# Per-tile centring and scaling on GpSimd, reciprocal roots by Newton steps for four streams at once, and the bias within the weights

## The reference

```python
def step(h, _):
    h = h + 0.01 * jnp.tanh(h)
    h = h * jax.nn.sigmoid(h)
    h = _layernorm(h, ln_w, ln_b)        # (h - mean) * rsqrt(var + 1e-5) * w + bias
    h = jnp.einsum('bsc,dc->bsd', h, W) + b
    return (h, None)
x, _ = jax.lax.scan(step, x, None, length=N_ITERS)   # N_ITERS = 30
```

## Time and profile before

| what | value |
|---|---|
| time, median of 3 runs | 2552.14 us (2551.59 to 2553.27) |
| profiled execution | 2566.49 us, span 2564.7 us |
| PE busy | 2378.7 us, 93% |
| PEld busy | 2320.6 us, 90% |
| DVE busy | 2081.9 us, 81% |
| POOL busy | 2027.5 us, 79% |
| ACT busy | 1811.9 us, 71% |
| L1094 products of the iterations, PE | 7680 matmuls, 275 ns each |
| L512 roots, POOL | 480, 1636 ns each |
| L515 scaling, POOL | 480, 1475 ns each |
| L661 statistics, DVE | 1920, 418 ns each |
| L704 state update, DVE | 464, 1209 ns each |
| L683 scaling, DVE | 960, 372 ns each |
| L957, L964, L967, ACT | 480, 464, 480; 1012, 1037, 1068 ns each |

### The profile page before, as it was taken

One profiled execution on the slowest core, in us unless ns is written; L12 is line 12 of the kernel. 1 busy time (PEld: TensorE's weight loads), 2 busy tenths in 40 slices (PEclk: granted clock), 3 DMA queues, 4 the chain that ended last, 5 costly groups with the idle time before them and its releaser, 6 DMA issues.

```text
span 2564.7 us, 60894 instructions
## 1 busy us (share of the span) xinstructions
PE 2378.7 (93%) x19678; PEld 2320.6 (90%) x19935; DVE 2081.9 (81%) x5761; ACT 1811.9 (71%) x2185; POOL 2027.5 (79%) x1592
## 2 busy tenths in 40 slices
PE   6829999999999999999999999999862999999998
PEld 5829999999999999999999999989861999999998
DVE  5999999999999999999999999987572444444443
ACT  3779999999999999999999999833210334344333
POOL 4769999999999999999999999995764444444443
PEclk9969999999999999999999999999885999999999
DMA  9100000000000000000000000003223555555554
GB/s 261 69 1 1 0 0 0 0 0 0 0 0 0 0 0 0 0 0 0 0 0 0 0 0 0 0 18 110 75 73 109 212 216 212 211 214 216 212 212 148
DMA packets 121574, 164.56 MB, mean 64 GB/s; under 512 B 14982, under 2 KB 74018, under 8 KB 121360
## 3 DMA queue, kind: packets, MB, share of 16 engines
q1 hardware_dynamic: 111792, 145.12, 16.6%
q0 software_dynamic: 9088, 17.14, 2.0%
q10 hardware_dynamic: 608, 1.30, 0.2%
HBM read 40.40 MB, written 24.65 MB: 25 GB/s over the span
## 4 chain that ended last, share of the span: by engine, by line
DVE 58%; PE 31%; issue 7%; POOL 1%; DMA 1%; ACT 1%; SPq 1%; another core or an unknown queue 0%; DVEq 0%; POOLq 0%; ACTq 0%
DVE pair_stats L661 25%; DVE state L704 18%; PE psum L1265 11%; PE psum L1256 11%; DVE state L683 6%; PE psum L1094 5%; PE psum L1084 2%; DVE it_vars L665 2%; DVE x_stats L661 1%; POOL sorted_rows L556 1%; DVE resid L731 1%; PE psum L1213 1%; DMA sorted_rows<-state,slot 1%; PE psum L1246 1%; DVE state L700 1%
## 5 line engine op out<-in xcount | busy, mean ns | idle before, releaser
L1094 PEld LDWEIGHTS psum<-w_ffn,turned 128*128 128x128 f32 x7680 | 1010.1, 192 | 36.0
L1094 PE MATMUL psum<-w_ffn,turned 128*128 128x128 f32 x7680 | 1013.7, 275 | 12.8 <-issue 0.2
L512 POOL TENSOR_TENSOR it_rstd<-it_vars,minus_half 128x8 f32<-128x8 f32 x480 | 785.5, 1636 | 0.0
L515 POOL TENSOR_TENSOR state<-state,it_rstd 128x768 f32<-128x768 f32 x480 | 708.0, 1475 | 37.6
L661 DVE BATCH_NORM_STATS2 pair_stats<-state 128x6 f32<-128x256 f32 x1920 | 685.1, 418 | 0.0
L1084 PE MATMUL psum<-ident,state 128*128 128x128 f32 x4352 | 595.6, 281 | 59.1 <-DVE state L700 42.8
L704 DVE SCALAR_TENSOR_TENSOR state<-state,psum 128x1024 f32<-128x1024 f32 x464 | 560.8, 1209 | 1.8 <-ACT state L964 0.9
L1084 PEld LDWEIGHTS psum<-ident,state 128*128 128x128 f32 x4352 | 479.5, 143 | 78.0 <-issue 57.7
L957 ACT COPY turned<-psum 128x1024 f32<-128x1024 f32 x480 | 485.8, 1012 | 80.4 <-PE psum L1084 43.9
L967 ACT ACTIVATE state<-state 128x1024 f32<-128x1024 f32 x480 | 512.7, 1068 | 28.6 <-DVE state L700 9.1
L964 ACT ACTIVATE state<-psum 128x1024 f32<-128x1024 f32 x464 | 481.0, 1037 | 0.0
(11 more groups left out here) (190 smaller groups left out, 1725.2 us busy)
## 6 DMA issues: line engine op xcount, KB each, us to landing
adjT<-resid SPq DMA_DIRECT2D x312, 320.0 KB
adjT<-sorted_rows SPq DMA_DIRECT2D x156, 66.5 KB, 1.8
resid<-in_x_dram SPq DMA_DIRECT2D x16, 512.0 KB, 7.3
state<-in_adj_dram SPq DMA_DIRECT2D x16, 512.0 KB, 7.3
adjT_dram<-adjT SPq DMA_DIRECT2D x7, 512.0 KB, 3.7
adjT<-adjT_dram SPq DMA_DIRECT2D x7, 512.0 KB, 3.5
out_dram<-resid,adjT POOLq DMA_INDIRECT x156, 2.4
sorted_rows<-state,slot POOLq DMA_INDIRECT x128
```

The lines of the kernel that those rows point to most:

```text
L512: nc.gpsimd.tensor_tensor(it_rstd[s % 8][:, :], it_vars[s % 4][:, :], minus_half[:, 0:TILES], ALU.pow).then_inc(it_pow, 1)
L515: nc.gpsimd.tensor_tensor(values[s][:, 0:POOL_TILES, :], values[s][:, 0:POOL_TILES, :], wide(it_rstd[s % 8][:, 0:POOL_TILES]), ALU.mult).t ...
L1094: last = nc.tensor.matmul(dst[:, t, :], stationary(t), moving(t), start=bias is None and m == 0, stop=m == len(terms) - 1, skip_group_chec ...
```

## The change

The statistics are kept in one tile for all 16 streams (`it_moments`), and `variance` and L683 go from DVE's iteration. POOL now works in batches of four streams. It waits for the statistics of all four, and computes the reciprocal roots of 4 x 8 = 32 columns at once from the sum of squares: one addition of 128 x eps, one multiplication by -0.5/128, a first guess by integer arithmetic on the bits, then three Newton steps of four instructions. That is 15 instructions, 14 of which have a wait for their own completion behind them. A one-column instruction (`pool_tick`) follows. Then each of the 8 tiles of each of the four streams gets one `tensor_scalar` with two per-row operands, subtract the mean and multiply by the root: 32 instructions of 128x128.

The bias matmuls of the iterations go. Instead, the copy after the transposition adds 1.0 to every value, and the bias / 128 is added to every row of the weights: the 128 ones then sum the bias, the ones times the centred weights sum to zero, and the centred rows times the constant bias / 128 sum to zero as well. For odd streams DVE copies tiles 0 to 3 of the eight and ACT the other four; even streams stay with ACT. PE waits for DVE's part too when the stream is odd.

```diff
-        SILU_LAG, STATS_LAG, SCALE_LAG, FLIP_LAG, EVAC_LAG = 1, 2, 5, STREAMS - 3, STREAMS - 2
-        POOL_TILES = 6
+        SILU_LAG, STATS_LAG, FLIP_LAG, EVAC_LAG = 1, 2, STREAMS - 3, STREAMS - 2
...
-            def iteration(base):
-                for s in range(STREAMS):
-                    pool.wait_ge(it_var, base + (s + 1))
-                    nc.gpsimd.tensor_tensor(it_rstd[s % 8][:, :], it_vars[s % 4][:, :], minus_half[:, 0:TILES],
-                                            ALU.pow).then_inc(it_pow, 1)
-                    pool.wait_ge(it_pow, base + (s + 1))
-                    nc.gpsimd.tensor_tensor(values[s][:, 0:POOL_TILES, :], values[s][:, 0:POOL_TILES, :],
-                                            wide(it_rstd[s % 8][:, 0:POOL_TILES]), ALU.mult).then_inc(it_scaled, 1)
+            ROOT_STEPS = 15
+
+            def roots(b, first):
+                v, h = it_vars[b % 2][:, 0, :], it_vars[b % 2][:, 1, :]
+                y, w = it_rstd[b % 2][:, :], it_work[b % 2][:, :]
+                at = [0]
+
+                def linked(ins):
+                    at[0] += 1
+                    ins.then_inc(it_root, 1)
+                    pool.wait_ge(it_root, first + (b * ROOT_STEPS + at[0]))
+
+                squares = it_moments[:, BATCH * b:BATCH * (b + 1), :, :].rearrange("p s i (h e) -> p (s i) h e", h=2)
+                linked(nc.gpsimd.tensor_tensor(halves(v), squares[:, :, :, 2], halves(root_const[:, 0, :]), ALU.add))
+                nc.gpsimd.tensor_tensor(h, v, root_const[:, 1, :], ALU.mult).then_inc(it_root, 1)
+                at[0] += 1
+                linked(nc.gpsimd.tensor_scalar(y.bitcast(I32), v.bitcast(I32), -0.5,
+                                               float(0x5f3759df + (7 << 22)), ALU.mult, ALU.add))
+                for _ in range(3):
+                    linked(nc.gpsimd.tensor_tensor(w, y, y, ALU.mult))
+                    linked(nc.gpsimd.tensor_tensor(w, w, h, ALU.mult))
+                    linked(nc.gpsimd.tensor_tensor(w, w, root_const[:, 2, :], ALU.add))
+                    linked(nc.gpsimd.tensor_tensor(y, y, w, ALU.mult))
+                assert at[0] == ROOT_STEPS
+
+                nc.gpsimd.tensor_tensor(pool_tick[:, :], minus_one[:, 0:1], minus_one[:, 0:1], ALU.mult)
+
+            def iteration(base, first):
+                for b in range(STREAMS // BATCH):
+                    pool.wait_ge(it_stats, base + BATCH * (b + 1))
+                    roots(b, first)
+                    for j in range(BATCH):
+                        s = BATCH * b + j
+                        for t in range(TILES):
+                            at = 3 * (t % 2) + 1
+                            mean = it_moments[:, s, t // 2, at:at + 1]
+                            root = it_rstd[b % 2][:, TILES * j + t:TILES * j + t + 1]
+                            last = nc.gpsimd.tensor_scalar(values[s][:, t, :], values[s][:, t, :], mean, root,
+                                                           ALU.subtract, ALU.mult)
+                        last.then_inc(it_scaled, 1)
...
+            nc.vector.scalar_tensor_tensor(w_ffn[:, :], crow[:, 1, 0:D], 1.0 / D, w_ffn[:, :], ALU.mult, ALU.add)
...
                     if n is not None:
                         dve.wait_ge(silu_done, n + 1)
-                        statistics(pair_stats[s % 4], values[s]).then_inc(it_stats, 1)
-                    if m is not None:
-                        dve.wait_ge(it_pow, m + 1)
-                        for t in range(POOL_TILES, TILES):
-                            last = nc.vector.tensor_scalar(values[r][:, t, :], values[r][:, t, :],
-                                                           it_rstd[r % 8][:, t:t + 1], None, ALU.mult)
-                        last.then_inc(it_scaled_v, 1)
-                    if n is not None:
-                        dve.wait_ge(it_stats, n + 1)
-                        variance(it_vars[s % 4][:, :], pair_stats[s % 4]).then_inc(it_var, 1)
+                        statistics(it_moments[:, s], values[s]).then_inc(it_stats, 1)
+                    if m is not None and r % 2 == 1:
+                        dve.wait_ge(it_flip, m + 1)
+                        nc.vector.tensor_scalar(turned[r % 4][:, 0:4, :], ring[r % 4][:, 0:4, :], 1.0, None, ALU.add
+                                                ).then_inc(it_turned_v, 2)
...
-                        nc.scalar.copy(turned[s % 4], ring[s % 4]).then_inc(it_turned, 1)
+                        own = slice(0, TILES) if s % 2 == 0 else slice(4, TILES)
+                        nc.scalar.activation(turned[s % 4][:, own, :], ring[s % 4][:, own, :], ACT.Copy, bias=1.0
+                                             ).then_inc(it_turned, 1)
...
                         pe.wait_ge(it_scaled, n + 1)
-                        pe.wait_ge(it_scaled_v, n + 1)
...
                         pe.wait_ge(it_turned, m + 1)
-                        rows(ring[r % 4], [(lambda t: turned[r % 4][:, t, :], lambda t: w_ffn[:, :])], bias=0
+                        if r % 2 == 1:
+                            pe.wait_ge(it_turned_v, m + 1)
+                        rows(ring[r % 4], [(lambda t: turned[r % 4][:, t, :], lambda t: w_ffn[:, :])]
                              ).then_inc(product, 1)
```

More of the change, by code:

```diff
@@ L108, in network @@
         shift = [sb(f"shift{j}", [P, 2, TILES]) for j in range(4)]
-        it_vars = [sb(f"it_vars{j}", [P, TILES]) for j in range(4)]
-        it_rstd = [sb(f"it_rstd{j}", [P, TILES]) for j in range(8)]
+        BATCH = 4
+        it_moments = sb("it_moments", [P, STREAMS, TILES // 2, 6])
+        it_vars = [sb(f"it_vars{j}", [P, 2, BATCH * TILES]) for j in range(2)]
+        it_rstd = [sb(f"it_rstd{j}", [P, BATCH * TILES]) for j in range(2)]
+        it_work = [sb(f"it_work{j}", [P, BATCH * TILES]) for j in range(2)]
+        root_const = sb("root_const", [P, 3, BATCH * TILES])
+        pool_tick = sb("pool_tick", [P, 1])
         row_vars = [sb(f"row_vars{j}", [P, TILES]) for j in range(4)]
@@ L161, in network @@
         h_bias = sb("h_bias", [P, 3, GW], BF16)
-        bias_mv = [sb(f"bias_mv{j}", [P, 4, P], BF16) for j in range(2)]
+        bias_mv = sb("bias_mv", [P, 4, P], BF16)
         def part(t, first, n):
@@ L468, in _ @@
             nc.gpsimd.memset(h_bias[:, :, :], 0.0)
-            for j in range(2):
-                nc.gpsimd.memset(bias_mv[j][:, :, :], 0.0)
+            nc.gpsimd.memset(bias_mv[:, :, :], 0.0)
+            nc.gpsimd.memset(root_const[:, 0, :], D * EPS)
+            nc.gpsimd.memset(root_const[:, 1, :], -0.5 / D)
+            nc.gpsimd.memset(root_const[:, 2, :], 1.5)
             nc.gpsimd.memset(mean_mat, 1.0 / D)
@@ L523, in _ @@
+            iteration(0, 0)
+            with pool.Fori(1, ITERS, 1) as i:
+                iteration(i * STREAMS, i * (STREAMS // BATCH * ROOT_STEPS))
             first = 0
@@ L648, in _ @@
                                       cpart[row, piece, 0, :].unsqueeze(1).to_broadcast([1, 3, GW]))
-                for j in range(2):
-                    last = nc.vector.tensor_copy(bias_mv[j][row, :, :],
-                                                 cpart[row, piece, 1 + j, 0:D].unsqueeze(1).to_broadcast([1, 4, P]))
+                last = nc.vector.tensor_copy(bias_mv[row, :, :],
+                                             cpart[row, piece, 2, 0:D].unsqueeze(1).to_broadcast([1, 4, P]))
             link(last)
@@ L1085, in flip, with rows @@
                 return last
-            def rows(dst, terms, bias=None):
+            def rows(dst, terms, bias=False):
                 for bank in range(2):
-                    if bias is not None:
-                        nc.tensor.matmul(dst[:, 4 * bank:4 * bank + 4, :], ones_bf[:, :], bias_mv[bias][:, :, :],
+                    if bias:
+                        nc.tensor.matmul(dst[:, 4 * bank:4 * bank + 4, :], ones_bf[:, :], bias_mv[:, :, :],
                                          start=True, stop=False, skip_group_check=True)
@@ L1094, in rows @@
                             last = nc.tensor.matmul(dst[:, t, :], stationary(t), moving(t),
-                                                    start=bias is None and m == 0, stop=m == len(terms) - 1,
+                                                    start=not bias and m == 0, stop=m == len(terms) - 1,
                                                     skip_group_check=True)
@@ L1202, in _ @@
                     rows(psM, [(lambda t: turned[d % 3][:, t, :], lambda t: w_mix[:, 0, :]),
-                               (lambda t: mask[:, t, :], lambda t: values[d][:, t, :])], bias=1).then_inc(mix_psum, 1)
+                               (lambda t: mask[:, t, :], lambda t: values[d][:, t, :])], bias=True).then_inc(mix_psum, 1)
                 if f is not None:
```

10 lines of the change are left out of this document (3 added, 7 removed).

## The result

The changed kernel takes 4626.0 us (median of 4 runs, 4624.4 to 4626.9), the kernel before 2551.9 in the same comparison: ratio 1.813, 95% interval 1.811 to 1.816. Forecast were 2690 us within 2430 to 3150: the sign is right, the size is far outside the range.

What follows compares the result with a forecast made beforehand. POOL was taken to bound the kernel before and after: 120 batches of 4.8 + 32 x 0.28 us, less 1510.3, plus 3.5, less 6.7, give +137.7 on 2552.1, so 2690 us, range 2430 to 3150.

Steps and rivals of the forecast that it cites:

- the price of the tile instruction: POOL's 128x128 tensor_scalar, taken as 0.28 us from the affine select's 0.25 plus 0.03 for two pointers.
- Ends 0.14 and 0.39: Limits for the tile instruction's spacing: a MEMSET's 0.14 us below, ACT's same-shaped instruction with two pointers, 0.39, above.
- T: Start-to-start spacing of POOL's 128x128 tensor_scalar instructions, forecast at 0.28 us; each 0.01 us is 38 us of time.
- (b): Rival, much slower: each pointer operand costs POOL a fetch before the tile; 0.39 us spacing, 3113 us; chance 0.21 with (d).
- POOL bounds the kernel before: In the iterations POOL holds the period at 3.14 us a slot (one stream, one iteration), three engines just behind.
- Roots of a batch: POOL's fifteen root instructions and one tick per four streams: 4.8 us, fourteen links 0.32 us apart.
- PE without the bias 2.65 us a slot, DVE 2.78, the half copy 0.6: Relieved engines per slot: PE 3.09 less 0.44, DVE 1.35 + 1.13 + 0.30; half copy every other slot.
- Start +3.5, end -6.7: Ends of POOL's iterations: first batch waits for four streams' statistics, +3.5 us; spare time before router products absorbs 6.7.
- A batch comes in time: POOL's batch has 7 and 10 slots, over 22 us, before PE's transposes need its first and last streams.
- Rival (a): Faster: tile instruction cheaper than any reading one in the trace, spacing below 0.244 us; about 2460 us, floor 2376; chance 0.27.
- Rival (d): PE's clock drops to 1.2 GHz as PE is busy 77%; +1030 us if held throughout; chance 0.21 with (b).

Runs made afterwards that it cites:

- f3: Kernel before with the batched Newton roots alone, POOL scaling seven tiles by one tensor_tensor, DVE one, nine slots behind; bias matmuls stay: 2559.1 us against 2566.4, ratio 0.997.
- g2: Kernel before with batched Newton roots, all eight tiles scaled on POOL, two Newton steps instead of three: 2524.4 us against 2552.2, ratio 0.989.
- f4: Changed kernel with only tile 0 of each stream centred and scaled on POOL, the other seven left as they are: 2383.2 us against 2566.4 before.
- e4: Changed kernel with each tile instruction handling only 64 of its 128 columns, both pointers kept: 3796.3 us.
- f1: Changed kernel with one two-operation tensor_scalar of 128x1024 with constants per stream instead of eight of 128x128 with pointers: 3394.8 us against 2566.4 before.
- h1: Changed kernel with one single-operation tensor_scalar of 128x1024 (multiply by constant 1.0) per stream instead of eight of 128x128: 2965.4 us.
- e1: Changed kernel with constants 0.0 and 1.0 instead of the mean and root pointers in the tile instruction: 3984.1 us.

## Why the prediction was wrong

The step that failed is the price of the tile instruction, "I take 0.28: the row of the same engine and width, and 0.03 for the pointers", with its ends, "Ends 0.14 and 0.39". T is 0.774. A batch has 32 of them and there are 120 batches, so this one term is (0.774 - 0.28) x 3840 = 1897 us of the 1936 that the forecast missed. The mechanism was right: POOL stays the bound, and its batches set the time. The size of one term of the sum was not. The runs put in its place

T = 0.18 fixed + 0.083 per pointer + columns x 2.5 ns (one operation) or x 3.4 ns (two),

which meets all seven measured values within 0.05 us (the 128-column ones within 0.01).

For 128 columns: 0.18 + 0.17 + 0.43 = 0.78. Of the 0.49 missed, about 0.14 are the pointers beyond the 0.03 allowed, 0.33 are the columns (0.43 against the 0.10 that the select's 0.25 leaves over the fixed 0.147), and the rest is the fixed part. What went wrong in the reasoning: the column's price was carried over from instructions that do other things (a MEMSET reads nothing, the select keeps a value or puts a constant), and the upper bound was built from tensor_tensor at 1.65 ns, as if one input must cost less than two. It costs more. Rows that disagree on a price by a factor of more than two (0.14, 0.25, 0.36, 0.39) were taken for a bracket, while the operation itself had never been seen on this engine. No rival had a dear column in it: (b), the nearest, stopped at 3113 us. Why one input with an operation is slower than two inputs stays open, and so does why the root part's own tensor_scalar (32 columns, integers, constants) lasts only 0.22 us.

Point by point:

- POOL bounds the kernel before: borne out, though hardly alone. With less work on POOL the slot fell from 3.14 only to 3.12 (f3, where DVE has no gap) and 3.09 (g2, where PE has none); the most that was gained is 28 us.
- Roots of a batch: 4.8 forecast, 4.95 measured. Links 0.33 apart instead of 0.32, in the first iteration, where the waits are against constants, as in the later ones, where they are against a register: the register costs nothing visible.
- PE without the bias 2.65 us a slot, DVE 2.78, the half copy 0.6: in f4 PE measured 2.67, DVE 2.77 and the half copy 0.59 from start to start. Right.
- Start +3.5, end -6.7: measured +1.6 and +4.8. Wrong in sign at the end: the prediction looked for what the new copies on DVE wait for in the middle of the iterations, and not at the wait ahead of them in the last one (DVE 68.33 us, PE 52.73). With the first batch, 9.5 us too long, it is some 20 us in 2074.
- A batch comes in time: right, POOL waits for statistics once, 3.54 us ahead of its first batch.
- Rival (b), pointers: it exists, 0.083 us each, and is a fifth of T. The rule of the Trainium skill, "GPSIMD Engine Reference", section Performance pitfalls for Q7 kernels, on small read commands (about 102 cycles, an estimated 0.085 us at its 1.2 GHz) has the same size; the page states it for reads such as one per gather index, and that a pointer operand is such a read no run shows. The same page of the Trainium skill, section Engine selection, says that one-input operations run roughly at line rate; that doesn't hold for this instruction: 3.4 and 2.5 ns a column (e4, f1, h1) would be an estimated 4 and 3 cycles at that clock, and both are above the 1.65 ns of two inputs. The measurement decides.
- Rival (a): nowhere near. Its floor, 176 us less, was met by f4 (183 less), once seven eighths of the tile work are gone.
- Rival (d), PE's clock: it did fall, to a granted 0.78, with PE busy 54% of the stretch, not the 77% at 1.00 that were forecast. It isn't in the loss, since PE waited over 3 us for POOL ahead of its transposes (3.32 and 3.33 above).

## What to carry to other kernels

When the whole sum hangs on the price of one operation that the trace doesn't show on that engine, rows of other operations are not bounds, not even a neighbouring one with more inputs; widen the range by a factor, or measure that one instruction first. Replacing one long instruction by eight short ones with per-row operands multiplies fixed and pointer costs by eight on an engine with no room; here that is 0.35 of each 0.774, and the price of the columns is the rest. And the gain of relieved engines (here 0.38 us a slot) is only what the new work on the bounding engine leaves of it.

## What the runs showed of the hardware that was not expected

- On GpSimd a tensor_scalar of float32 costs 2.5 ns a column with one operation and 3.4 with two, where tensor_tensor, one of its inputs broadcast, costs 1.65 (e1 to e4, f1, h1; the earlier trace rows). Each operand from a pointer adds 0.083 us.
- Two tensor_tensor of 128x1024 (3.85 us) do the work of eight two-operation tensor_scalar of 128x128 (6.2 us).
- A VectorE tile instruction of 0.27 us lasted up to 1.75 when a long GpSimd instruction was under way (f3); long instructions on GpSimd are dear for VectorE even where GpSimd isn't the bound. The other way round, a GpSimd instruction of 0.25 us lasted 1.11 beside a VectorE update with both inputs in SBUF (first batch of the changed kernel); beside the later updates, with one input in PSUM, none of the root part's is stretched (one update runs from 2018.41 to 2019.63, in the root part from 2014.70 to 2019.65).
